# Second half of a mixing layer moved from the table loop into the edge batches, on one Trainium2 core

## The chip, the cores and the metric

The kernel runs on one core of one Trainium2 chip. The metric is device time in microseconds (us) from the launch to the end of the program, as the median of several runs. Engines: PE is TensorE, DVE is VectorE, ACT is ScalarE, POOL is GpSimd, SP is SyncE, which here only issues transfers. Each engine runs its own instructions in order and waits on semaphores for the others.

## The reference

One layer of a graph network over 3125 nodes of 256 numbers and 50,000 edges, everything in fp32. With xn the layer-normed nodes:

- A graph attention: keys, values and queries by node type (6 types), a score for each edge, a softmax over all edges of a type, and a sum of the weighted values into each target node, then a layer norm.
- A mixing layer ("mix") on the same xn: q, k and v by one weight, elu(q)+1 and elu(k)+1, linear attention over all nodes; then

```python
x1 = layer_norm(t + x, ln1_g, ln1_b)
h = gelu(x1 @ W1.T + b1)
y = h @ W2.T + b2
return layer_norm(y + x1, ln2_g, ln2_b)
```

- The sum of x and both goes through a layer norm and a feed-forward block (256 to 1024 to 256) whose output counts only for the top 1561 nodes by a router weight.

The change is about the four lines of code above. All of it is computed as before in both kernels.

## The kernel before, in words

Nodes stand in NT = 25 tiles of 128 rows; sorted by type and padded they fill NS = 30 tiles. Edges stand in 98 groups of 4 x 128; two groups are a batch, so there are 49 batches.

The program has five stages, all of them written out by hand: each engine has one list of calls, and the order of the calls in that list is the order of its work. There is no planner.

1. Front (0 to 80 us): loads, the first layer norm, keys of the mix layer, edge indices turned.
2. Table loop (80 to about 290 us), 31 steps. Step s computes keys, values and queries of sorted tile s (`turn_in`, `keys_values`, `queries`, `by_type` on PE; POOL gathers the tile's rows and scatters two tables), and beside that one tile of the mix layer, skewed over six steps: `mix_q`, `mix_t`, `mix_turn` (L996), `mix_h` (L985), gelu on ACT (L794), `mix_y` (L1006, L1007), then `residual` and `finish` on DVE. `turn_in` (L896) and `queries` (L932) write the same PSUM bank, `ps[0]`, so `turn_in` of the next tile waits until DVE has read the queries (L1252). SP stores the finished rows to `mix_scratch`.
3. Edge batches (about 300 to 918 us). For a batch: POOL gathers 8 x 128 rows of keys and values (L1425) into a ring of 7 slots of four tiles, the seventh of which is the memory of the mix weights, `wmix`; a slot is free again when `window_sums` has read it. SP loads query windows (L1384) and key rows (L1393). ACT builds one-hot matrices (L1485, L1488, L1500, L1504), copies sums (L1522, L1528) and takes the exponentials (L1513). PE: `target_rows` (L1604), `window_sums` (L1621), `turn_sums` (L1630), `turn_maxima` (L1648), `spread_maxima` (L1655), `totals` (L1639). DVE: `products` (L1750), `head_sums` (L1757), maxima, `weights` (L1800), `messages` (L1809), and one step of a search over nodes (L1853).
4. Combine (918 to 984 us): stored sums are scaled (L2062) and multiplied (L2315), chunks are stored and gathered back.
5. Feed-forward, selection and output (984 to 1167 us): PE L2351 and L2364; DVE prepares rows two tiles at a time in `normalise_pair`, reading `rows`, which were loaded from `mix_scratch`.

In the edge stage one iteration of the PE list is, in order: target_rows, turn_sums, turn_maxima, window_sums, spread_maxima, turn_sums, totals, target_rows, window_sums. The functions that the change touches, with the lines of the profile:

Of the kernel before, what the change touches and what calls it, by code (L numbers as in the profile page):

```python
# [15 lines left out]
P = 128  # L16
N, D = 3125, 256
C = D // P
# [14 lines left out]
RING = 7  # L33
RING_BIG = RING - 1
# [9 lines left out]
SEARCH_AT = 6  # L44
SEARCH_STEPS = 4 + NT + 4
# [11 lines left out]
STATS_AT = (13, 14, 15)  # L57
T_AT = 1
# [17 lines left out]
def build(nc, a, out):  # L76
# [6 lines left out]
    mix_d = scratch("mix_scratch", (NP, D))  # L83
    agg_d = scratch("agg_scratch", (AR, D))
# [5 lines left out]
    with ExitStack() as ctx:  # L90
# [27 lines left out]
        wqT, w1T, w2T = (wmix[:, i * C * D:(i + 1) * C * D].rearrange("p (c o) -> p c o", c=C) for i in range(3))  # L118
        vec_names = ["L0_gnn_ln_g", "L0_gnn_ln_b", "L0_mix_ln2_g", "L0_mix_ln2_b", "L0_mix_b2", "L0_ffn_b2",
# [33 lines left out]
        edge = Arena("edge", 7808)  # L153
# [70 lines left out]
        hT = big.take(2, D)  # L224
        assert big.at <= rel_end
        big.reset(xs_at)
        x2m = big.take(2, D)
        mo = big.take(2, D)
        den = big.take(2, H)
        sts, mvs, rss = big.take(4, 6), big.take(4, 2), big.take(4, 2)  # L230
        nmr = big.take(2)
        x1g = big.take(3, D)
# [16 lines left out]
        kv_slots = [kv[:, s, :, :] for s in range(RING_BIG)] + [wmix[:, :].rearrange("p (k d) -> p k d", k=EG)]  # L249
# [11 lines left out]
        gap = edge.take(4, 64)  # L261
        edge.reset()
# [24 lines left out]
        rows_c = edge.take(NT, D)  # L287
        selT = edge.take(C, ETY, P)
# [10 lines left out]
        junk = edge.take(NHG)  # L299
        edge.reset()  # L300
# [11 lines left out]
        same_t = [vecs[name][0:HW, 0:NHG] for name in ("L0_mix_ln2_g", "L0_mix_ln2_b")]  # L312
        base_f = vecs["L0_mix_b2"][:, 0:NHG + 1]
# [107 lines left out]
        def type_marks(c, dve, in_t, tmp):  # L421
            for t in range(ETY):
# [30 lines left out]
        m_q, m_min, m_exp, m_kf, m_t, m_tx, m_r1, m_rs, m_xh, m_T, m_x1, m_h, m_g, m_y, m_c, m_r2, m_out = (  # L453
            sem(n) for n in ("mix_q", "mix_min", "mix_exp", "mix_kf", "mix_t", "mix_tx", "mix_rstd_1", "mix_shift", "mix_xh",
                             "mix_turned", "mix_x1", "mix_h", "mix_gelu", "mix_y", "mix_stats_2", "mix_rstd_2", "mix_out"))
        m_xin = pair("mix_x_in")
        vmx, pmx, m_xg = sem("mix_step"), sem("mix_pool_step"), sem("mix_x1_gained")
        N_VEC = 5
        mix_vecs = ["L0_mix_b2", "L0_mix_ln2_g", "L0_mix_ln2_b", "L0_gnn_ln_b"]
        mix_vecs += [name for name in vec_names if name in ("L0_mix_ln1_g", "L0_mix_ln1_b")]  # L460
        late_vecs = [name for name in vec_names if name not in mix_vecs]
# [4 lines left out]
        with nc.Block() as block:  # L466
            @block.sync
            def _(sp):
# [80 lines left out]
                seen_all(sp, m_st, NT, 16)  # L549
                sp.wait_ge(s_late, 16 * N_LATE)  # L550
# [6 lines left out]
            def _(pool):  # L557
# [94 lines left out]
                def roots(t, ready, done, n):  # L652
                    if t is None:
                        return
                    seen(pool, ready, t)
                    j = 2 * n + t.k
# [3 lines left out]
                def gained(t):  # L660
                    if t is None:
                        return
                    if t.t == 0:
                        pool.wait_ge(s_pri, 1)
                    seen(pool, m_xh, t)
                    seen(pool, m_c, t.at(-3))
                    pool.tensor_tensor(x1g[:, t.t % 3, :], xh[:, t.k, :], vecs["L0_mix_ln1_g"][:, :], ALU.mult).then_inc(m_xg, 1)

                load(Tile(0, 0, NS))
                load(Tile(0, 1, NS))  # L670
                for s in range(NS + 1):
                    t, m = Tile(s // 2, s % 2, NS), Tile(s // 2, s % 2, NT)
                    roots(m.at(-5), m_c, m_r2, 1)
                    gained(m.at(-2))
                    load(t.at(2))
                    store_kv(t.at(0))
                    roots(m.at(-1), m_tx, m_r1, 0)
# [1958 lines left out]
```

## Time and profile before

| | us |
|---|---|
| median of three runs | 1170.04 |
| the three runs | 1173.99, 1167.43, 1170.04 |
| span of the profiled execution, its own time as far as the profile has it | 1167.3 |
| PE busy | 967.1 (83%) |
| DVE busy | 803.3 (69%) |
| POOL busy | 640.5 (55%) |
| ACT busy | 587.4 (50%) |

The span runs from the first to the last instruction of the profiled execution; the median of the timed runs is 2.7 us longer. Busy time is a sum over the whole span, so it hides that the stages differ: the profile's slices show PE full and at full clock in the table loop and in the feed-forward part, and at 0.5 to 0.7 of full clock in the edge batches.

### The profile page before, as it was taken

The numbers are of one execution on the slowest core, as the hardware profiler recorded it, in microseconds if no ns is written. First come the engines' busy times: TensorE is split into PE (matmuls) and PEld (weight loads), VectorE is DVE, ScalarE is ACT, GpSimd is POOL, SyncE is SP. The second block draws the span as 40 slices with busy tenths as digits, with TensorE's granted clock in tenths as the row PEclk, the third lists the DMA queues.
The fourth block names the chain that finished last, engine by engine and source line by source line (L and its number), as shares of the span: only waits on it lengthen the run. The fifth ranks groups of instructions, "written<-read, shape, count | busy, mean of one in ns | idle before, by whom it ended". The sixth has DMA issues, their size and how long they took to land.

```text
span 1167.3 us, 18084 instructions
## 1 busy us (share of the span) xinstructions
PE 967.1 (83%) x5053; PEld 677.5 (58%) x5053; DVE 803.3 (69%) x1708; ACT 587.4 (50%) x1534; POOL 640.5 (55%) x818
## 2 busy tenths in 40 slices
PE   5989999997157788777877878778778898999998
PEld 4767777775034444444444444444444687888886
DVE  7755888885256777777767677776767677887541
ACT  2657999983234554555545455554555322322220
POOL 4516788886725666666656666565664025664000
PEclk9999999999565766666667666666776799999999
DMA  9722544444736776766767767677674274210020
GB/s 294 220 71 104 159 145 145 146 146 174 234 114 182 208 212 210 205 204 203 214 202 214 210 198 211 201 211 208 201 211 146 69 226 152 79 46 19 1 86 25
DMA packets 112091, 189.89 MB, mean 163 GB/s; under 512 B 18187, under 2 KB 80734, under 8 KB 111990
## 3 DMA queue, kind: packets, MB, share of 16 engines
q0 software_dynamic: 38992, 129.87, 36.1%
q1 hardware_dynamic: 69718, 55.57, 15.7%
q10 hardware_dynamic: 3280, 3.28, 0.8%
q8 instruction: 43, 0.70, 0.2%
q14 instruction: 58, 0.48, 0.1%
HBM read 154.21 MB, written 34.44 MB: 162 GB/s over the span
## 4 chain that ended last, share of the span: by engine, by line
PE 55%; ACT 12%; issue 11%; another core or an unknown queue 10%; DVE 9%; DMA 1%; SPq 1%; POOL 0%; DVEq 0%; ACTq 0%; POOLq 0%
PE ps L2364 7%; PE ps L1621 7%; PE ps L2351 7%; PE ps L1604 6%; PE ps L921 4%; ACT edge L1500 4%; PE ps L2315 3%; PE ps L932 2%; PE ps L909 2%; PE ps L960 2%; ACT edge L1488 2%; PE ps L985 2%; ACT edge L1485 1%; PE ps L1639 1%
## 5 line engine op out<-in xcount | busy, mean ns | idle before, releaser
L1425 POOL DMA_INDIRECT big<-kv_scratch,src_i x336 | 317.8, 946 | 203.0 <-issue 89.8
L1604 PE MATMUL ps<-edge 64*128 64x256 f32 x784 | 177.6, 595 | 39.0 <-issue 38.8
L1750 DVE TENSOR_TENSOR big<-big,ps 128x1024 f32<-128x1024 f32 x84 | 101.6, 1210 | 121.3 <-PE ps L1604 61.9
L1621 PE MATMUL ps<-big,edge 128*64 128x256 f32 x672 | 149.4, 590 | 19.3 <-issue 10.3
L1604 PEld LDWEIGHTS ps<-edge 64*128 64x128 f32 x784 | 104.7, 289 | 89.5 <-issue 75.1
L1522 ACT ACTIVATE edge<-ps 128x256 f32<-128x256 f32 x98 | 37.6, 383 | 213.3 <-remote 146.0
L1621 PEld LDWEIGHTS ps<-big,edge 128*64 128x64 f32 x672 | 63.2, 199 | 78.6 <-issue 70.0
L1500 ACT ACTIVATE edge<-edge 128x64 f32<-128x64 f32 x392 | 102.9, 334 | 0.0
L1757 DVE TENSOR_REDUCE ps<-big 128x32 f32<-128x1024 f32 x84 | 102.3, 1218 | 0.1
L1809 DVE TENSOR_TENSOR big<-big,ps 128x1024 f32<-128x1024 f32 x84 | 98.9, 1209 | 0.0
L2351 PE MATMUL ps<-big 128*128 128x256 f32 (+2 forms) x416 | 88.7, 368 | 2.8 <-ACT big L2264 2.8
L2364 PE MATMUL ps<-big 128*128 128x256 f32 (+1 forms) x400 | 90.0, 380 | 0.0
L2277 ACT ACTIVATE big<-ps,fb 128x256 f32<-128x256 f32 (+2 forms) x104 | 39.4, 461 | 99.8 <-PE ps L2351 99.8
L1630 PE MATMUL ps<-ident,edge 128*128 128x128 f32 x196 | 53.6, 365 | 41.2 <-ACT edge L1522 32.7
L2351 PEld LDWEIGHTS ps<-big 128*128 128x128 f32 x416 | 74.3, 190 | 11.8 <-ACT big L2264 2.7
L2364 PEld LDWEIGHTS ps<-big 128*128 128x128 f32 (+1 forms) x400 | 73.6, 188 | 10.6 <-issue 0.3
L1425 POOL DMA_INDIRECT wmix<-kv_scratch,src_i x56 | 53.1, 948 | 30.8 <-issue 15.0
L1488 ACT ACTIVATE edge<-edge,ones 128x256 f32<-128x256 f32 x98 | 49.8, 508 | 29.4 <-remote 20.3
L1630 PEld LDWEIGHTS ps<-ident,edge 128*128 128x128 f32 x196 | 23.4, 168 | 68.7 <-ACT edge L1522 51.3
L921 PE MATMUL ps<-big,edge 128*128 x120 | 56.9, 596 | 0.5 <-ACT edge L727 0.3
L1485 ACT ACTIVATE edge<-edge,iota_n 128x256 f32<-128x256 bf16 x98 | 48.7, 497 | 13.9 <-DMA edge<-key_scratch 13.8
L1504 ACT ACTIVATE edge<-edge,ones 128x256 f32<-128x256 f32 x98 | 49.8, 508 | 8.9 <-issue 0.4
(354 smaller groups left out, 1919.0 us busy)
## 6 DMA issues: line engine op xcount, KB each, us to landing
edge<-q_scratch SPq DMA_DIRECT2D x196, 64.0 KB
edge<-key_scratch SPq DMA_DIRECT2D x98, 64.0 KB
big<-kv_scratch,src_i POOLq DMA_INDIRECT x336
agg_scratch<-big SPq DMA_DIRECT2D x16, 252.0 KB
xn_scratch<-big ACTq DMA_DIRECT2D x5, 640.0 KB, 5.4
mix_scratch<-big SPq DMA_DIRECT2D x25, 128.0 KB
big<-xn_scratch SPq DMA_DIRECT2D x25, 128.0 KB, 2.6
edge<-in_x SPq DMA_DIRECT2D x24, 128.0 KB
```

The lines of the kernel that those rows point to most:

```text
L921: ins = pe.matmul(ps[1][:, :], xgT[:, t.k, ch * P:(ch + 1) * P], wall[:, ds(ty, 1), ch, 0:2 * D].rearrange("p a o -> p (a o)"), start=(ch ...
L1425: pool.indirect_dma_start(kv_slots[s][:, k, :], None, kv_d[0:N, :], bass.IndirectOffsetOnAxis(ap=src_i[:, e:e + 1], axis=0)).then_inc(got[ ...
L1488: act.activation(ohT[:, g % 2, :], dist, ACT.Relu, bias=ones[:, 0:1], scale=-1.0).then_inc(oh, 1)
L1500: ins = act.activation(gap[:, 2 * k + hg, :], iota_m, ACT.Abs, bias=neg_key[:, e:e + 1])
L1604: ins = pe.matmul(qr_ps[g % 2][:, (2 * hg + k) * D:(2 * hg + k + 1) * D], ohT[64 * hg:64 * hg + 64, g % 2, k * P:(k + 1) * P], qwin[64 * h ...
L1621: ins = pe.matmul(sums_of(g)[64 * hg:64 * hg + 64, :], oneh[:, s, k, hg * 64:hg * 64 + 64], kv_slots[s][:, 2 * hg + k, D:2 * D], start=(k ...
L1630: ins = pe.transpose(sums_of(g)[:, ch * P:(ch + 1) * P], rows_of_sums(g)[:, ch * P:(ch + 1) * P], ident[:, :])
L1750: dve.tensor_tensor(k_rows, k_rows, qr_ps[g % 2].rearrange("p (k d) -> p k d", d=D), ALU.mult).then_inc(pr, 1)
L1757: dve.tensor_reduce(scr[:, g // 2 % 2, (g % 2) * EG * H:(g % 2 + 1) * EG * H].rearrange("p (k h) -> p k h", h=H), kv_slots[g % RING][:, :, ...
L1809: dve.tensor_tensor(v, v, wgt[:, g // 2 % 2, (g % 2) * EG * H:(g % 2 + 1) * EG * H] .rearrange("p (k h d) -> p k h d", h=H, d=1).to_broadc ...
L2351: ins = pe.matmul(hslot[q % 2][:, j * GT * P:j * GT * P + w], fw1[:, ch, f * P:(f + 1) * P], cols[:, ch, at:at + w], start=(ch == 0), stop ...
L2364: ins = pe.matmul(ps[4 + t % 2][0:m, 0:D], fh[:, p % 2, f, at:at + m], fw2[:, f, :], start=(f == 0), stop=(f == FJ - 1))
```

## The change

- The second half of the mix layer (W1, gelu, W2, residual, second statistics) leaves the table loop. Instead SP stores x1, turned, to a new scratch tensor `x1_d`, one tile per step; `mo` is now only x plus a bias.
- In the edge stage each of the 25 tiles is spread over four iterations. Tile m starts at b = 7 + 3m//2: ACT issues the load of x1 one iteration before, PE does `mix_h` at b, ACT the gelu at b+1, PE `mix_y` at b+1 (now with the residual added by a product with the identity), DVE a row, statistics, variance and gain at b+1, ACT issues the store to `x2_d` at b+2.
- The mix weights stay in `wmix`, so the gather ring has 6 slots and not 7.
- In the table loop `turn_in` gets its own bank, `ps[7]`, and stands right behind `keys_values`; `queries` now waits for DVE's read instead. On DVE `attend` stands ahead of `q_bias_in`. POOL's `gained` and the second `roots` go, and its loads run three tiles ahead.
- In the combine stage POOL takes 25 reciprocal roots at once; SP loads the rows of `x2_d`, and DVE adds them with one instruction per tile, `prepare_row`.

```diff
-RING = 7
-RING_BIG = RING - 1
+RING = 6
+RING_BIG = RING
+MIX_FROM = [7 + 3 * m // 2 for m in range(NT)]
+X1_LAG, X2_LAG = -1, 2
...
 SP, table loop
+                    seen(sp, m_x1, t)
+                    sp.dma_start(x1_d[t.t, :, :], x1T[:, t.t % 3, :]).then_inc(m_x1st[t.k], 16)
...
 PE, table loop
-                    seen(pe, g_qc, t.at(-1))
+                    seen(pe, g_Tc, t.at(-1))
-                        ins = pe.transpose(ps[0][...], xg[...], ident[:, :])
+                        ins = pe.transpose(ps[7][...], xg[...], ident[:, :])
...
                     keys_values(t.at(0))
+                    turn_in(t.at(1))
                     mix_t(m.at(-1))
                     mix_turn(m.at(-2))
                     queries(t.at(0))
-                    mix_h(m.at(-3))
-                    turn_in(t.at(1))
                     by_type(t.at(-1))
-                    mix_y(m.at(-4))
...
 ACT, edge batches
+                def load_x1(m):
+                    at_least(act, yp, m - 1)
+                    act.dma_start(x1e[:, m % 2, :], x1_d[m, :, :]).then_inc(x1in[m % 2], 16)
+                def store_x2(m):
+                    act.wait_ge(yg, m + 1)
+                    act.dma_start(x2_d[m * P:(m + 1) * P, :], x2e[:, m % 2, :]).then_inc(x2st[m % 2], 16)
+                def mix_gelu(m):
+                    act.wait_ge(hp, m + 1)
+                    at_least(act, yp, m)
+                    for j in range(C):
+                        ins = act.activation(hTe[...], h_ps_e[...], ACT.Gelu, bias=b1c[:, j:j + 1])
+                    ins.then_inc(hk, 1)
...
                         distances(2 * b + 2)
+                    for m in mix_tiles(b, X1_LAG):
+                        load_x1(m)
+                    for m in mix_tiles(b, 1):
+                        mix_gelu(m)
+                    for m in mix_tiles(b, X2_LAG):
+                        store_x2(m)
                     keep_rows(2 * b - 3)
...
 PE, edge batches
+                def mix_h(m):
+                    pe.wait_ge(x1in[m % 2], 16 * (m // 2 + 1))
+                    at_least(pe, yr, m)
+                    (4 products of 128 x 128 x 128 into h_ps_e)
+                def mix_y(m):
+                    pe.wait_ge(hk, m + 1)
+                    (2 products of 128 x 128 x 256 and 4 of 128 columns into y_ps_e)
...
                     turn_sums(2 * b - 3)
+                    for m in mix_tiles(b, 1):
+                        mix_y(m)
                     totals(b - 1)
                     target_rows(2 * b + 2)
                     window_sums(2 * b - 2)
+                    for m in mix_tiles(b, 0):
+                        mix_h(m)
...
 DVE, edge batches
+                def mix_row(m):
+                    dve.wait_ge(yp, m + 1)
+                    at_least(dve, x2st[m % 2], 16 * (m // 2))
+                    dve.tensor_tensor(x2e[:, m % 2, :], y_ps_e, vecs["L0_mix_b2"][:, :], ALU.add).then_inc(yr, 1)
...
                     mark(b)
+                    mix_row(m)      (m of mix_tiles(b, 1))
                     messages(2 * b - 2)
+                    mix_stats(m)
                     messages(2 * b - 1)
+                    mix_var(m)
+                    mix_gain(m)
...
 DVE, combine and feed-forward
+                def prepare_row(i):
+                    dve.wait_ge(s_x2r, 2)
+                    dve.wait_ge(mix_in[i // 2 % 3], 16 * (i // 6 + 1))
+                    dve.wait_ge(x2in[i % 2], 16 * (i // 2 + 1))
+                    dve.scalar_tensor_tensor(rows[:, i, :], x2e[:, i % 2, :], x2r[:, i:i + 1], rows[:, i, :], ALU.mult, ALU.add)
```

## Rows read from the trace of the kernel before

**Rows 1.** Busy time by stretch: us, then PE, PEld, DVE, ACT, POOL, clock, DMA share, GB/s.
```profile
177.43:249.91 72.48, 72.48 (x482) 57.74 (x481) 59.84 (x171) 67.65 (x130) 58.34 (x80) 1.00 0.41 146
418.00:890.00 472.00, 373.91 (x1679) 207.88 (x1677) 343.75 (x505) 249.96 (x743) 295.36 (x313) 0.66 0.70 207
984.00:1100.00 116.00, 113.76 (x554) 99.33 (x553) 85.90 (x291) 33.26 (x90) 58.67 (x104) 1.00 0.15 45
```
**Rows 2.** PE timeline, one step of the table loop: start, us, instruction, count.
```profile
202.28 1.06 PE L985 MATMUL ps<-big,wmix 128*128 128x128 f32 x8
203.18 0.43 PE L896 MATMUL ps<-ident,edge 128*128 128x128 f32 x2
...
204.38 0.70 PE L1006 MATMUL ps<-wmix,big 128*128 128x256 f32 x2
...
205.35 1.05 PE L960 MATMUL ps<-big,wmix 128*128 128x128 f32 x8
```
**Rows 3.** Groups by line, ten steps of the table loop (177.43 to 249.91).
```profile
L658 POOL TENSOR_TENSOR big<-big,nhalf 128x1 f32<-128x1 f32 x20 | 12.7, 637 | 1.7
L642 POOL DMA_INDIRECT kv_scratch<-edge,big x10 | 11.9, 1189 | 3.1 <-issue 3.1
L667 POOL TENSOR_TENSOR big<-big,v_L_mix_ln_g 128x256 f32<-128x256 f32 x10 | 7.2, 716 | 0.0
L1308 DVE SCALAR_TENSOR_TENSOR big<-big,v_L_mix_ln_g 128x256 f32<-128x256 f32 x10 | 4.5, 455 | 0.0
```
**Rows 4.** ACT timeline of the same step: the gelu and the table load before it.
```profile
203.16 1.28 ACT L794 ACT_TABLE_LOAD   x1
204.46 0.63 ACT L794 ACTIVATE big<-ps,b1c 128x128 f32<-128x128 f32 x2
```
**Rows 5.** Timeline of an early step, before the loop holds mix_h and mix_y.
```profile
89.27 0.44 PE L896 MATMUL ps<-ident,edge 128*128 128x128 f32 x2 [0.73 <-DVE edge L1252]
```
**Rows 6.** DVE timeline: first instruction of batches 8, 47 and 48.
```profile
418.13 1.22 DVE L1750 TENSOR_TENSOR big<-big,ps 128x1024 f32<-128x1024 f32 x1 [2.55 <-remote]
...
889.64 1.22 DVE L1750 TENSOR_TENSOR big<-big,ps 128x1024 f32<-128x1024 f32 x1 [2.99 <-PE ps L1604]
...
898.30 1.21 DVE L1750 TENSOR_TENSOR big<-big,ps 128x1024 f32<-128x1024 f32 x1
```
**Rows 7.** Who waited for whom, 418 to 890: us in total, times, longest.
```profile
DVE big L1750 <- PE ps L1604: 60.3, 20, 3.8
...
DVE big L1750 <- remote: 35.5, 14, 3.1
```
**Rows 8.** Timeline of batch 10, all engines (start, us, instruction, idle before).
```profile
444.72 0.51 ACT L1488 ACTIVATE edge<-edge,ones 128x256 f32<-128x256 f32 x1
...
445.50 0.38 ACT L1522 ACTIVATE edge<-ps 128x256 f32<-128x256 f32 x1 [0.27 <-issue]
...
446.54 0.36 ACT L1513 ACTIVATE edge<-edge 128x192 f32<-128x192 f32 x1 [0.66 <-issue]
...
447.39 1.13 PE L1604 MATMUL ps<-edge 64*128 64x256 f32 x8
...
448.11 2.33 DVE L1809 TENSOR_TENSOR big<-big,ps 128x1024 f32<-128x1024 f32 x2
...
450.37 0.41 DVE L1853 SCALAR_TENSOR_TENSOR edge<-v_L_mix_b,edge,step_f 128x196 f32<-128x196 f32 x1
...
454.15 1.22 DVE L1750 TENSOR_TENSOR big<-big,ps 128x1024 f32<-128x1024 f32 x1 [3.36 <-PE ps L1604]
```
**Rows 9.** Timeline at the end of batch 25, PE at full clock.
```profile
631.59 1.13 PE L1604 MATMUL ps<-edge 64*128 64x256 f32 x8
...
632.22 0.95 POOL L1425 DMA_INDIRECT big<-kv_scratch,src_i  x1 [0.30 <-issue]
...
635.53 0.44 PE L1630 MATMUL ps<-ident,edge 128*128 128x128 f32 x2 [2.81 <-ACT edge L1522]
```
**Rows 10.** One transfer issued from ACT, in the front: ns, min/median/max.
```profile
L694 ACTq DMA_DIRECT2D xn_scratch<-big x5: 366/382/440, 27.0 to 64.8; - x5
```
**Rows 11.** DVE timeline in the combine stage: one instruction of `gained`, then the next scale.
```profile
963.81 0.48 DVE L2429 SCALAR_TENSOR_TENSOR big<-big,v_L_gnn_ln_g 128x256 f32<-128x256 f32 x1
964.21 2.26 DVE L2062 TENSOR_TENSOR big<-big 128x756 f32<-128x756 f32 x2
```

More of the change, by code:

```diff
@@ L57 @@
 STATS_AT = (13, 14, 15)
+X2_AT = (14, 15)
 T_AT = 1
@@ L261, in build @@
         gap = edge.take(4, 64)
+        base_f = edge.take(NHG + 1)
+        hTe = edge.take(D)
+        x2s = edge.take(6)
+        assert edge.at <= NT * D + 32
         edge.reset()
@@ L287, in build @@
         rows_c = edge.take(NT, D)
+        edge.take(32)
         selT = edge.take(C, ETY, P)
@@ L299, in build @@
         junk = edge.take(NHG)
+        same_last = edge.take(NHG)
         edge.reset()
@@ L786, in affine @@
                     ins.then_inc(m_x1, 1)
-                def gelu(t):
-                    if t is None:
-                        return
-                    seen(act, m_h, t)
-                    seen(act, m_y, t.at(-2))
-                    for j in range(C):
-                        ins = act.activation(hT[:, t.k, j * P:(j + 1) * P], ps[7][:, j * P:(j + 1) * P], ACT.Gelu,
-                                             bias=b1c[:, j:j + 1])
-                    ins.then_inc(m_g, 1)
                 for s in range(NS + 1):
@@ L801, in _ @@
                     elu(m.at(0))
+                    weights(t.at(1))
+                    turn_in(t.at(1))
                     affine(m.at(-2))
-                    weights(t.at(1))
-                    gelu(m.at(-3))
-                    turn_in(t.at(1))
                     q_out(t.at(-1))
@@ L929, in queries @@
                     seen(pe, g_w, t)
+                    seen(pe, g_qc, t.at(-1))
                     for o in range(C):
@@ L1369, in build, with mix_tiles @@
             fac_ps = [ps[7][:, 0:ETY * NB], ps[0][:, 0:ETY * NB]]
+            h_ps_e, y_ps_e = ps[0][:, 0:D], ps[0][:, D:2 * D]
+            def mix_tiles(b, lag):
+                return [m for m in range(NT) if MIX_FROM[m] + lag == b]
             def in_range(g):
@@ L2035, in build @@
                 "scaled_first", "scaled_second", "rows_ps", "rows_kept"))
-            ck_st, mix_in = pair("rows_stored"), sem("mix_in")
+            ck_st, mix_in = pair("rows_stored"), [sem(f"x_rows_in{j}") for j in range(3)]
+            x2in, rp = pair("x2_in"), sem("rows_prepared")
+            s_x2r = sem("x2_rstds")
             s_fw, s_head, s_tails = sem("ffn_weights_in"), pair("heads_in"), pair("tails_in")
@@ L2132, in _ @@
                 load_part(1)
+                for i in range(2):
+                    sp.wait_ge(x2st[i], 16 * ((NT + 1 - i) // 2))
+                load_x2(0)
+                load_x2(1)
                 for k in range(NU):
@@ L2164, in _ @@
                 sp.wait_ge(s_totalst, 32)
-                for t in range(GR, NT):
-                    load_xn(t)
+                for t in range(4, NT):
+                    if t + 4 >= GR and t + 4 < NT:
+                        load_xn(t + 4)
+                    load_x2(t)
                 for t in range(NT):
```

177 lines of the change are left out of this document (94 added, 83 removed).

## The prediction

> **What bounds the kernel now.** I read the slices of the page first, then busy time by stretch, then for each stage a timeline of one step, and last who waited for whom.
>
> The table loop is bound by PE. In ten steps, 72.48 us, PE is busy for all 72.48 at clock 1.00, so a step costs 7.25 us; ACT has 67.65 and DVE and POOL about 59 each [rows 1]. Whatever leaves PE there shortens the step until the next engine is full.
>
> The edge batches are not bound by any engine. From batch 8 at 418.13 to batch 47 at 889.64 a batch takes 471.51 / 39 = 12.09 us [rows 6], with PE busy 79%, DVE 73%, POOL 63% and ACT 53% of the stretch [rows 1]. In a batch DVE runs without a break from its first product (batch 10: 442.04, that is 12.1 before 454.15) to the search step at 450.37 + 0.41, and then sits idle 3.36 us [rows 8]. Over the stretch these waits are 60.3 + 35.5 us [rows 7], about 2.5 us a batch. What DVE waits for is strange: target_rows started at 447.39 and took 1.13 us, so it was done at 448.5, yet DVE went on only at 454.15 [rows 8]. PE's speed is not it: in batch 25 PE ran at the higher of its two clock levels, its last product was done at 631.59 + 1.13 = 632.7, and it idled 2.81 us until ACT freed it at 635.5 [rows 9]. What ends at that time is the gathers: the last one was issued at 632.22, 2.9 us earlier. And batch 47, when the last gathers are out, takes 898.30 - 889.64 = 8.66 us [rows 6]. So a batch has about 3 us in which DVE and ACT have nothing to do, and PE's signals seem to be seen late as long as gathers are under way. That slack is the cover for the moved work, and the prediction turns on how much of the work fits under it.
>
> The feed-forward part is bound by PE again (113.76 of 116 us), with DVE at 85.90 [rows 1].
>
> **The table loop.** mix_h occupies PE from 202.28 to 203.18, 0.90 us; mix_y from 204.38 to 205.35, 0.97 us [rows 2]. Together 1.87 us of 7.25, which leaves 5.38. Would another engine be fuller than that? POOL: 5.83 a step [rows 1], less 0.72 for the gain, 0.64 for a root and 0.25 (estimate, the addition before it) is 4.2, and with three gaps like the 0.31 behind each indirect transfer [rows 3] 5.1: just under. ACT: 6.77 less two table loads of 1.28 and the gelu's 0.63 [rows 4] (there is no second table left in the loop, so the load back to exp goes too) is 3.6. DVE: 5.98 less four instructions of about 0.45 [rows 3] and smaller ones is under 4. So PE stays the bound, near 5.4; I take 5.5, because POOL is so close. That is 1.75 for each of the 21 steps that hold both parts, 37 us. The first four steps hold neither, but PE idles 0.73 us there waiting for DVE's read of the shared bank [rows 5]; its own bank ends that: 3 us. Of the last steps, which hold the tail of the mix layer, four lose 1.87 us of PE, but there POOL's scatters are close: I take 5. Sum -45. Bounds: -30, if POOL holds the step at 6.1; -53, if PE is all there is. The extra store of x1 lies on SP, which has its queue otherwise for one load and one store a step; nothing, up to 2.
>
> **The edge batches: where the work goes.** Of three batches, two hold a mix_h and two a mix_y. The iteration with mix_y is the dear one, for everything in it is one chain. I put it on batch 10, whose first product is at 442.04:
>
> - ACT is free at 444.72 + 0.51 = 445.23 [rows 8]. Now a table load 1.28, the gelu 0.63 [rows 4], one transfer issued, 0.38 [rows 10] (the load of x1 or the store of x2): 447.5. Then keep_rows, 0.38, done 447.9 instead of 445.88; then the table load back, 1.28, and the exponentials 0.36: done at 449.55 instead of 446.90 [rows 8]. So 2.65 us late, and weights and messages stand behind them on DVE.
> - PE: turn_sums waits for keep_rows, 448.4. mix_y is 0.97 and its four products with the identity half of mix_h, 0.45: 1.4 at full clock, 449.8; at the lower level 2.8, 451.2. totals, target_rows and window_sums are queued behind it, and POOL's next gathers behind window_sums.
> - DVE: weights and mark end about 450.3; mix_row waits for mix_y. Then mix_row 0.46, first message 1.17, statistics 0.46, second message 1.17, variance 0.2, gain 0.46, search 0.41: 4.3 us. Next product at 454.6 (full clock) or 455.6 (lower level), against 454.15 now.
>
> So if signals came at once, such a batch would cost 0.5 to 1.5 us, because the 3.36 us of idle time hide the rest. But mix_y stands exactly ahead of totals and target_rows, whose signals reach nobody before 454 [rows 8]. If DVE saw mix_y as late as it now sees target_rows, at 454.0, the 4.3 us would start there: 458.3, or 4.2 us more. The two ends are 0.5 and 4.2 us per tile. I take 2.4, about the middle: the nearest row (target_rows) is for the high end, but the turn_sums just ahead of mix_y is seen in time to let ACT go on in the same batch. 25 x 2.4 = 60 us; bounds 12 and 105.
>
> The page on the table load has a different price. By the rows the gelu starts 1.30 us after its table load [rows 4]. The Trainium skill, ScalarE: Activation LUTs, What ACT_TABLE_LOAD costs, gives about 1380 ns of drain on top of the 1283 ns for every switch; by that rule two switches a tile would bring exponentials 2.76 us later still, and 25 tiles 69 us more. The trace shows no such drain between the two instructions, and the sum goes by the trace.
>
> mix_h stands behind the last window_sums and ahead of target_rows, whose result DVE needs only 3 us into the next batch: 0.9 to 1.8 us of PE, in the stretch in which PE has work left or idles for signals. I take 0.3 a tile, 7 us; bounds 0 and 45 (all of it on the chain). Stores and loads of 128 KB, three a tile, ride beside 207 GB/s [rows 1]; counted in the same term. The ring of 6: a gather is released by the same window_sums as now, one group nearer to its use. Its product comes at least 2 us after it lands in steady batches, so nothing; up to 5 us in the first batches.
>
> **After the batches.** prepare_row is one more DVE instruction of 0.48 us [rows 11] per tile. Three stand between scales of the combine stage, where DVE is on the chain: 1.4. In the feed-forward part DVE goes from 85.90 to about 85.90 + 16 x 0.48 = 93.6 of 116 us [rows 1]: it fits, with some waits: 2. Sum 3; bounds 1 and 10.
>
> **Sum.** -45 + 60 + 7 + 3 = +25 us on the span's 1167.3, 1192; the median of the runs is 2.7 above the span: 1195.
>
> **Rivals.**
>
> 1. The slack takes it all (the side on which it is faster). Signals of mix_y come at once, batches with mix_y cost 0.8 us and the next batch gives half back, since POOL's gathers restart before DVE: 25 x 0.6 = 15, mix_h nothing. 1170 - 45 + 15 + 3 = 1143; with less luck 1155. For it: 95.8 us of DVE waits in the stretch [rows 7]; ACT idle for half of it. Against it: the chain ACT, PE, DVE in the iteration is serial and already fills the slack with nothing over. It decides from 1.4 us a tile down.
> 2. mix_y is seen only when the gathers have landed: 25 x 4.2 = 105, so 1170 - 45 + 105 + 7 + 3 = 1240. For it: target_rows in every steady batch. Against it: turn_sums, two instructions ahead, is not held so long.
> 3. The table loop doesn't shrink as it should (POOL's order with three transfers and one root pair, or the DVE read that queries now waits for): gain 20 and not 45, 1220. Against it: no engine but PE is over 5.1.
> 4. The page's drain at each table switch: 1264. Against it: the trace.
>
> **How the numbers follow.** A measurement of this kernel can't tell less than about 0.5% (6 us) from no change. Forecast 0.47 (its own range 1160 to 1225: 0.01 of it faster, 0.06 within 0.5%, 0.40 slower); rival 1 0.30 (0.26 faster, 0.04 within); rival 2 0.16; rival 3 0.05; rival 4 0.02, all slower. Faster 0.27, same 0.10, slower 0.63. The range must reach into rivals 1 and 2: 1145 to 1245.
>
> **What would show it.** The step of the table loop between 5.3 and 5.6 us with PE still full and only one or no ACT table load in it. In the batches: periods of 12.1 for iterations without mix_y and 13.5 to 16 for those with it; exponentials about 2.7 us later there; DVE's idle time in front of L1750 gone and new idle time in front of mix_row, on mix_y. If mix_row waits until the last gather has landed, rival 2 is right. If batches stay at 12.1 to 12.6 throughout, rival 1 is. The forecast is wrong if the edge stage grows by less than 35 us.

## The result, and the profile after

The changed kernel takes 1154.84 us (median of 4 runs, 1152.96 to 1161.79) against 1168.74 for the kernel before on the same chip: ratio 0.9891, 95% interval 0.9859 to 0.9923. It is 1.1% faster, where 1195 was forecast. The profiled execution has a span of 1151.2 us against 1167.3. A second measurement on another chip (below) gave 0.9876, 0.9826 to 0.9925. Executions over 1.5% above the fastest of the same kernel are left out of the ratios, so a ratio can differ a little from the quotient of two medians.

The table loop first. One step is the distance between two `keys_values` (PE timeline: start, us, instruction, count), and the first row below is ten steps by stretch, as [rows 1].

```profile
133.87:188.29 54.42, 54.42 (x361) 40.89 (x361) 36.93 (x111) 37.66 (x90) 39.59 (x51) 1.00 0.62 218
```
```profile
139.15 1.88 PE L913 MATMUL ps<-big,edge 128*128 x4
140.87 0.38 PE L888 MATMUL ps<-ident,edge 128*128 128x128 f32 x2
144.59 1.88 PE L913 MATMUL ps<-big,edge 128*128 x4
146.31 0.38 PE L888 MATMUL ps<-ident,edge 128*128 128x128 f32 x2
```
The step is 5.44 us (was 7.25), and PE is still busy for all of it.

Then where the edge batches begin in the two kernels: batch 0 of before, then batches 0, 8, 26 to 29, 47 and 48 of after (DVE timeline). Batch 26 holds mix_y and mix_h (yh), 27 mix_y only (y), 28 mix_h only (h), and so on in threes.

```profile
301.86 1.22 DVE L1750 TENSOR_TENSOR big<-big,ps 128x1024 f32<-128x1024 f32 x1 [0.80 <-issue]
```
```profile
252.10 1.22 DVE L1765 TENSOR_TENSOR big<-big,ps 128x1024 f32<-128x1024 f32 x1 [0.50 <-issue]
...
363.01 1.22 DVE L1765 TENSOR_TENSOR big<-big,ps 128x1024 f32<-128x1024 f32 x1 [2.32 <-remote]
...
595.17 1.22 DVE L1765 TENSOR_TENSOR big<-big,ps 128x1024 f32<-128x1024 f32 x1 [1.96 <-remote]
...
608.89 1.22 DVE L1765 TENSOR_TENSOR big<-big,ps 128x1024 f32<-128x1024 f32 x1
...
620.80 1.22 DVE L1765 TENSOR_TENSOR big<-big,ps 128x1024 f32<-128x1024 f32 x1
...
632.05 1.22 DVE L1765 TENSOR_TENSOR big<-big,ps 128x1024 f32<-128x1024 f32 x1 [2.50 <-remote]
...
858.93 1.22 DVE L1765 TENSOR_TENSOR big<-big,ps 128x1024 f32<-128x1024 f32 x1 [3.56 <-PE ps L1594]
...
870.92 1.22 DVE L1765 TENSOR_TENSOR big<-big,ps 128x1024 f32<-128x1024 f32 x1 [2.79 <-remote]
```
From batch 8 to 47 a batch takes (858.93 - 363.01) / 39 = 12.72 us, against 12.09 [rows 6]. The three in the middle take 13.72 (yh), 11.91 (y) and 11.25 (h). Over batches 8 to 43 the means of the twelve of each kind are 15.0, 12.7 and 10.5: a yh batch costs 2.9 us more than a batch of before, a y batch 0.6 more, and the h batch that ends the three is 1.6 us shorter than one. (One yh batch, 14, takes 19.9; with a ring of 6 it is long also without the moved work, 15.9 and 16.0. Without it the yh mean is 14.5.)

DVE's time splits these 24.4 us (495.92 against 471.51) by simple subtraction. DVE is busy for 379.4 us of this stretch and was for 343.4: 36.0 more, 1.4 a tile. Its idle time fell only from 128.1 to 116.5. In front of `products` it fell from 108 to 15 us, but new waits took its place: 17 us in front of mix_row, 19 in front of the reduction that waits for the exponentials (L1815), 18 in front of `maximum` (L1801), and most, 45, in front of `subtract`, which waits for PE's `spread_maxima`. The largest part of those (363 to 859: us, times, longest):
```profile
DVE edge L1808 <- remote: 25.3, 14, 2.3
```
By kind, DVE is idle 4.4 us in a yh batch, 2.5 in y and 1.8 in h, against 3.3 in a batch of before.

Last, what the combine stage waits for. These are PE's first combine matmul in before and in after, DVE's longest total wait in that stage of after (us, times, longest), and the rows of DVE and SP around its two stalls.

```profile
920.71 0.55 PE L2315 MATMUL ps<-bd_m,big 128*126 128x128 f32 x1 [1.45 <-DVE big L2062]
```
```profile
892.25 0.97 PE L2374 MATMUL ps<-bd_m,big 128*126 128x128 f32 x3 [1.45 <-DVE big L2102]
```
```profile
DVE edge L2495 <- DMA wmix<-mix_x_scratch: 13.8, 2, 8.9
```
```profile
939.25 0.50 SPq L2160 DMA_DIRECT2D wmix<-mix_x_scratch  x1
...
944.39 0.48 DVE L2495 SCALAR_TENSOR_TENSOR edge<-wmix,v_L_mix_ln_b,edge 128x256 f32<-128x256 f32 x1 [4.92 <-DMA wmix<-mix_x_scratch]
...
964.95 0.42 SPq L2160 DMA_DIRECT2D wmix<-mix_x_scratch  x1
...
967.23 0.48 DVE L2495 SCALAR_TENSOR_TENSOR edge<-wmix,v_L_mix_ln_b,edge 128x256 f32<-128x256 f32 x1 [8.87 <-DMA wmix<-mix_x_scratch]
```
`prepare_row` waits for its x2 rows, and SP issues their load only at 939.25 and 964.95, because the loads stand in its queue behind stores and waits for totals. From the first combine matmul to the end it is 1151.2 - 892.25 = 259.0 us, against 1167.3 - 920.71 = 246.6.

So the 16.1 us by which the span is shorter are made up as follows: the first product comes 49.8 us earlier; batches 0 to 7 take 5.4 less (116.3 to 110.9); batches 8 to 46 take 24.4 more; batch 47 to the first combine matmul 2.3 more (31.1 to 33.3); the rest 12.4 more.

### The profile page after: what moved, and what is told of

Its sections match the earlier page's. It is cut to its first block, busy times and chain, and to the rows that moved or that the text cites. A ratio compares the mean times of both kernels' runs of the same rounds, so it can differ in the third digit from the quotient of the medians.

```text
span 1151.2 us, 18271 instructions
## 1 busy us (share of the span) xinstructions
PE 925.1 (80%) x5153; PEld 678.8 (59%) x5153; DVE 790.9 (69%) x1682; ACT 598.7 (52%) x1540; POOL 600.2 (52%) x745
## 4 chain that ended last, share of the span: by engine, by line
PE 45%; DVE 17%; issue 14%; ACT 10%; POOL 5%; another core or an unknown queue 4%; DMA 3%; SPq 1%; DVEq 0%; ACTq 0%; POOLq 0%
PE ps L1611 7%; PE ps L1594 5%; PE ps L2423 5%; PE ps L913 4%; PE ps L2410 4%; DVE big L1824 4%; PE ps L954 2%; PE ps L2374 2%; PE ps L925 2%; PE ps L901 2%; ACT edge L1466 2%; DVE big L1765 2%; POOL big L2272 2%; PE ps L1620 2%
## 5 line engine op out<-in xcount | busy, mean ns | idle before, releaser
L1389 POOL DMA_INDIRECT big<-kv_scratch,src_i x392 | 370.9, 946 | 257.5 <-PE ps L1611 120.8
L1594 PE MATMUL ps<-edge 64*128 64x256 f32 x784 | 145.2, 501 | 35.3 <-issue 22.5
L1611 PE MATMUL ps<-big,edge 128*64 128x256 f32 x784 | 138.1, 485 | 31.0 <-issue 13.8
L1765 DVE TENSOR_TENSOR big<-big,ps 128x1024 f32<-128x1024 f32 x98 | 118.5, 1209 | 44.1 <-remote 34.5
L1594 PEld LDWEIGHTS ps<-edge 64*128 64x128 f32 x784 | 86.6, 238 | 62.1 <-issue 50.2
L1772 DVE TENSOR_REDUCE ps<-big 128x32 f32<-128x1024 f32 x98 | 119.4, 1218 | 0.1
L1824 DVE TENSOR_TENSOR big<-big,ps 128x1024 f32<-128x1024 f32 x98 | 116.6, 1208 | 0.0
L1620 PE MATMUL ps<-ident,edge 128*128 128x128 f32 x196 | 49.5, 341 | 70.3 <-ACT edge L1488 60.9
L2410 PEld LDWEIGHTS ps<-big 128*128 128x128 f32 x416 | 77.8, 201 | 12.5 <-ACT big L2323 2.7
L1454 ACT ACTIVATE edge<-edge,ones 128x256 f32<-128x256 f32 x98 | 49.8, 508 | 23.9 <-remote 10.4
L2374 PE MATMUL ps<-bd_m,big 128*126 128x128 f32 (+1 forms) x396 | 49.3, 289 | 7.9 <-DVE big L2102 6.9
L1808 DVE TENSOR_TENSOR edge<-edge,ps 128x192 f32<-128x192 f32 x49 | 17.2, 351 | 55.4 <-remote 31.0
```

The lines of the kernel that those rows point to most:

```text
L1389: pool.indirect_dma_start(kv_slots[s][:, k, :], None, kv_d[0:N, :], bass.IndirectOffsetOnAxis(ap=src_i[:, e:e + 1], axis=0)).then_inc(got[ ...
L1594: ins = pe.matmul(qr_ps[g % 2][:, (2 * hg + k) * D:(2 * hg + k + 1) * D], ohT[64 * hg:64 * hg + 64, g % 2, k * P:(k + 1) * P], qwin[64 * h ...
L1611: ins = pe.matmul(sums_of(g)[64 * hg:64 * hg + 64, :], oneh[:, s, k, hg * 64:hg * 64 + 64], kv_slots[s][:, 2 * hg + k, D:2 * D], start=(k ...
L1620: ins = pe.transpose(sums_of(g)[:, ch * P:(ch + 1) * P], rows_of_sums(g)[:, ch * P:(ch + 1) * P], ident[:, :])
L1765: dve.tensor_tensor(k_rows, k_rows, qr_ps[g % 2].rearrange("p (k d) -> p k d", d=D), ALU.mult).then_inc(pr, 1)
L1772: dve.tensor_reduce(scr[:, g // 2 % 2, (g % 2) * EG * H:(g % 2 + 1) * EG * H].rearrange("p (k h) -> p k h", h=H), kv_slots[g % RING][:, :, ...
```

## The experiments

The kernel before had medians between 1168.6 and 1177.5 us beside these runs, so all comparisons are between ratios to it; 0.01 is 12 us. The changed kernel's own is 0.989 and 0.988.

**The yardstick.** The changed kernel, unedited, run late in the series.

> The changed kernel once more, unedited, beside the same runs of the kernel before, as the yardstick for the ratios of the other experiments. If the ratio does not depend on the chip it is 0.989 (0.986 to 0.992); if it does, the comparisons of the experiments with the changed kernel shift by the difference.

Measured: 0.9876 (0.9826 to 0.9925). The ratio holds, and the interval says that less than about 6 us can't be told between two experiments.

**The x2 loads earlier.**
```
-X2_AT = (14, 15)
+X2_AT = (13, 14, 16)
...
-                    load_x2(t)
+                    if t >= 2 + len(X2_AT):
+                        load_x2(t)
```


> The changed kernel, with the loads of the stored x2 rows of tiles 2, 3 and 4 issued earlier on SP's queue (behind the stores of units 13, 14 and 16, ahead of the waits for head rows and totals). In the changed kernel DVE stands still 4.92 us from 939.5 and 8.87 us from 958.4 waiting for exactly these loads. Theory A (those two stalls are the 12 us by which the part behind the batches grew): both go, 10 to 14 us faster, about 1142. Theory B (the gathers of sums or POOL's roots are as late as the loads, so another wait takes their place): 0 to 3 us faster, 1152 to 1155.

Measured: 1148.96, ratio 0.9735 (0.9699 to 0.9772), 16 to 18 us faster than the changed kernel by the ratios, 12 to 14 by the medians (1148.96 / 1175.85 = 0.977). DVE's waits for these loads over the same stretch of the profile:
```profile
DVE edge L2496 <- DMA wmix<-mix_x_scratch: 5.8, 2, 3.3
```
They fell from 13.8 to 5.8, and the part behind the first combine matmul (at 898.43 of a span of 1147.8) from 259.0 to 249.4, 2.8 us over the 246.6 of before. Theory A. The profiles show 9.6 us of the gain; the rest is within what the intervals leave open. It is the version with the lowest ratio that leaves nothing out.

**The moved work left out of the batches.**
```
             def mix_tiles(b, lag):
-                return [m for m in range(NT) if MIX_FROM[m] + lag == b]
+                return []
```


> The changed kernel with the moved second half left out of the edge batches altogether (no loads of x1, no products, gelu, row work or stores; the combine stage reads other rows of the same size in place of x2). Theory A (the moved work costs what the batches grew, 12.72 - 12.09 = 0.63 us a batch): batches of 12.1 us, about 25 us faster, 1130. Theory B (the moved work does cost 2.4 us a tile, 60 us, as forecast, and something else in the changed kernel made the batches shorter at the same time, such as the clock that rose from 0.66 to 0.80): batches of 10.5 to 11.2 us, 50 to 70 us faster, about 1095.

Measured: 0.9689 (0.9663 to 0.9715), 23 us faster than the changed kernel. Its batches 8 and 47 begin at:
```profile
362.28 1.22 DVE L1765 TENSOR_TENSOR big<-big,ps 128x1024 f32<-128x1024 f32 x1 [2.69 <-PE ps L1594]
...
844.27 1.22 DVE L1765 TENSOR_TENSOR big<-big,ps 128x1024 f32<-128x1024 f32 x1 [3.83 <-PE ps L1594]
```
That is 12.36 us a batch, against 12.87 for the kernel with earlier x2 loads on the same chip. Theory A: the moved work really costs only 0.9 us a tile net, with whatever the changed clock gives back in it, and no other part of the change hid a larger price.

**The ring alone, in the kernel before.**
```
-RING = 7
-RING_BIG = RING - 1
+RING = 6
+RING_BIG = RING
```
(and the slot in `wmix` taken off the list.)

> The kernel before with a ring of six gathered groups in place of seven, and nothing else. Theory A (the ring only sets when the last gathers fall): batches stay at 12.09 us, the one in which the last gathers land moves by one (batch 47 12 us and not 8.66): 3 to 4 us slower, about 1172. Theory B (the ring of six is itself what lengthened the batches by 0.63 us): 20 to 25 us slower, about 1192.

Measured: 0.9993 (0.9974 to 1.0012). Batches of 12.29 us, and the last one with gathers takes 11.96 us, not 8.66, as A says; on the whole time even that can't be seen. On the same chip the changed kernel without the moved work had 12.36. Theory B is out.

**Half the gathers, before and after.**
```
-                    for k in range(EG):
+                    for k in range(0, EG, 1 if g < RING else 2):
...
-                    dve.wait_ge(got[u], 64 * (g // RING + 1))
+                    dve.wait_ge(got[u], 64 + 32 * (g // RING))
```


> The kernel before with every second gather of the edge batches left out after the first seven groups (POOL issues 4 a batch in place of 8, 1.25 us each; the rows that are left stay from earlier groups). In the run with plain copies for the gelus four different results of PE became visible together at 572.9, 2.0 us after the last gather had been issued. Theory A (PE's signals are held back while gathers are under way, and that sets the period of 12.1 us): batches of about 8.7 us, as the one batch behind the last gathers, 130 us faster, about 1040. Theory B (the 12.1 us have to do with something else, PE's work at its lower clock level or the key and query windows that SP loads): 11 to 12 us a batch, less than 45 us faster.

Measured: 1036.44, ratio 0.8817 (0.8779 to 0.8855), 139 us faster. Theory A. Its batches 8 and 47:
```profile
397.94 1.22 DVE L1750 TENSOR_TENSOR big<-big,ps 128x1024 f32<-128x1024 f32 x1
...
757.41 1.20 DVE L1750 TENSOR_TENSOR big<-big,ps 128x1024 f32<-128x1024 f32 x1
```
9.22 us a batch, and DVE is busy for 342.7 of these 359.5 us, 95%: now DVE is the bound. The run takes two things away at once, though: 5.0 us of POOL's own issuing a batch (four gathers, 1.25 us apart) and the late signals. In the kernel before, POOL's round adds up to the period: eight gathers from 442.27 to 451.96, then 2.42 us until the next starts, 12.1 in all (rows in the last section). How much of the 2.9 us is due to the late signals and how much to the issuing is not separated by any run.

And the changed kernel with the same gathers gone:

> The changed kernel with the same gathers left out. Theory A (a slack that the gathers make hides the moved work): without that slack every tile costs what its instructions take in the chain, 1.5 us on DVE and up to 2.6 us of later exponentials, 40 to 100 us over the 25 tiles, so this kernel comes out level with or slower than the one before with half its gathers, although its table loop is 50 us shorter. Theory B (the moved work costs 0.5 to 0.6 us a batch whatever the gathers do): 15 to 20 us faster than that one.

Measured: 1085.55, ratio 0.9242 (0.9204 to 0.9280): 50 us slower than the one above, though its table loop is 50 us shorter. First products of batches 8, 24 (y), 25 (h), 26 (yh), 27 and 47:
```profile
344.27 1.22 DVE L1765 TENSOR_TENSOR big<-big,ps 128x1024 f32<-128x1024 f32 x1
...
535.22 1.22 DVE L1765 TENSOR_TENSOR big<-big,ps 128x1024 f32<-128x1024 f32 x1
...
546.26 1.22 DVE L1765 TENSOR_TENSOR big<-big,ps 128x1024 f32<-128x1024 f32 x1
...
555.04 1.22 DVE L1765 TENSOR_TENSOR big<-big,ps 128x1024 f32<-128x1024 f32 x1
...
569.20 1.22 DVE L1765 TENSOR_TENSOR big<-big,ps 128x1024 f32<-128x1024 f32 x1
...
795.15 1.21 DVE L1765 TENSOR_TENSOR big<-big,ps 128x1024 f32<-128x1024 f32 x1
```
A mean of 11.56; y takes 11.04, h 8.78, yh 14.16. Without the slack the moved work costs (11.56 - 9.22) x 39 / 25 = 3.7 us a tile. With it, 1.0. Note that a yh batch takes about the same in both, by the medians 14.2 here and 14.3 with all gathers, while y and h batches have 11.2 and 8.8 here and 12.8 and 11.0 there. So the full gathers lengthen the y and h batches and hardly the yh ones. That a yh batch is one chain over the engines is my reading of it.

**The table loads, with and without the slack.**
```
-   ins = act.activation(hTe[...], h_ps_e[...], ACT.Gelu, bias=b1c[:, j:j + 1])
+   ins = act.activation(hTe[...], h_ps_e[...], ACT.Copy)
```


> The changed kernel with a plain copy in place of the gelu in the edge batches, so that ACT needs no other table there: the same instructions in the same places, two table loads of 1.28 us a tile less, and exponentials 2.6 us earlier in 25 batches. Theory A (the exponentials stand on the chain of a batch with mix_y, and the slack hides about half): 1.0 to 1.5 us a tile, 25 to 35 us faster, that is all of what the moved work costs. Theory B (DVE's own extra 1.5 us is what lengthens the batch, and the exponentials' lateness lies beside it): 0 to 8 us faster.

Measured with all gathers: 0.9901 (0.9864 to 0.9937), no gain at all.

> The changed kernel with every second gather left out and with plain copies in place of the gelus (no table loads in the edge batches). With all gathers the missing table loads gained nothing. Theory A (they lie on the chain of a batch and were hidden only by the gathers): 2.0 to 2.6 us a tile, 50 to 65 us faster than with half the gathers and the gelus, 1020 to 1035. Theory B (they lie beside DVE's work in any case): 0 to 15 us faster, 1070 to 1085.

Measured with half the gathers: 1039.42, ratio 0.8832 (0.8804 to 0.8859), 48 us faster than with the switches, 1.9 us a tile. The price is close to that of theory A (1.9 where it had 2.0 to 2.6), and the copies, 0.43 us for two against 0.63, are a small part of it. So in the first of the two B had the right number but not the reason: the loads are on the chain, and with all gathers something else takes their place. The trace of the kernel without switches shows what, in its yh batch that begins at 560.99:
```profile
567.07 1.06 PE L1669 MATMUL ps<-ident,wmix 128*128 128x128 f32 x4
...
569.97 0.94 POOL L1389 DMA_INDIRECT big<-kv_scratch,src_i  x1 [0.30 <-issue]
...
572.94 0.42 DVE L1909 TENSOR_TENSOR wmix<-ps,v_L_mix_b 128x256 f32<-128x256 f32 x1 [3.78 <-remote]
```
mix_y is done at 568.1 and mix_row starts at 572.94, 2.0 us behind the issue of the last gather. POOL had issued eight gathers without a break since 561.22. That is not every tile: of the 25 mix_row, DVE idled for "remote" ahead of five, 19.1 us in all, against one and 4.1 us in the changed kernel. In the changed kernel, with its table loads, the same place looks like this (batch 23, which begins at 557.02):
```profile
562.90 1.28 ACT L1510 ACT_TABLE_LOAD   x1
...
564.20 0.63 ACT L1510 ACTIVATE edge<-ps,b1c 128x128 f32<-128x128 f32 x2
564.21 0.35 DVE L1808 TENSOR_TENSOR edge<-edge,ps 128x192 f32<-128x192 f32 x1 [1.19 <-PE ps L1645]
...
564.40 0.95 POOL L1389 DMA_INDIRECT big<-kv_scratch,src_i  x1 [1.55 <-PE ps L1611]
...
566.29 0.61 PE L1670 MATMUL ps<-ident,wmix 128*128 128x128 f32 x4
566.41 0.36 ACT L1479 ACTIVATE edge<-edge 128x192 f32<-128x192 f32 x1
...
567.36 0.41 DVE L1910 TENSOR_TENSOR wmix<-ps,v_L_mix_b 128x256 f32<-128x256 f32 x1
567.69 1.21 DVE L1824 TENSOR_TENSOR big<-big,ps 128x1024 f32<-128x1024 f32 x1
```
mix_y is done at 566.9 and mix_row runs at 567.36, behind `mark`, with no wait of its own. POOL is issuing here too, but in a shorter run: it had paused until 564.40 for window_sums. By kind, the kernel without switches has 15.2, 12.1 and 12.0 where the changed one has 15.0, 12.7 and 10.5: the y batch gains, and the h batch gives back nothing any more.

**DVE's four steps spread.** mix_row behind the second messages; statistics, variance and gain in the next batch, ahead of `maximum`, `subtract` and `weights`; `X2_LAG` 3; with the earlier x2 loads.

> The changed kernel with the earlier x2 loads, and with DVE's four steps of a tile moved: mix_row behind the second messages of the batch, statistics, variance and gain into the next batch, each ahead of an instruction for which DVE stands idle there (maximum, subtraction, weights). Nothing is left out. Theory A (what a tile costs is DVE's own 1.5 us in a batch that DVE fills, and messages that stand behind a late signal of mix_y): batches of 12.4 to 12.6 us, 8 to 18 us faster than with the earlier loads alone, 0.96 of the time of before. Theory B (the cost is PE's work or the chain over the gelu ahead of the exponentials): within 3 us of the kernel with the earlier loads alone, 0.973.

Measured: 0.9754 (0.9705 to 0.9802), within 0.002 of the same without it; batches of 13.05 in the profile, whose execution was the longest of the six (1159.07). Not DVE's order, then, as theory B says, within the 6 us or so that the intervals leave open.

**Both edits together.**

> The kernel with the earlier x2 loads and DVE's steps spread, now also with plain copies for the gelus, so without table loads in the edge batches. Each of these two edits alone gained nothing with all gathers. Theory A (they cover for one another: without table loads the messages stood up to 3.8 us behind a late signal of mix_y, as at 572.94; with mix_row behind the messages that wait is off the chain): batches of 12.3 to 12.5 us, as with the moved work left out, 15 to 25 us faster than the spread kernel, ratio 0.955 to 0.962. Theory B (what is left of the cost has another cause, such as PE's work or late signals of target_rows and window_sums, which come later the more PE has to do): batches of 12.9 to 13.1, ratio 0.972 to 0.977.

Measured: 1137.83, ratio 0.9734 (0.9691 to 0.9776). The profile has batches of 12.54 against 12.86 of the changed kernel on the same chip, close to the 12.3 to 12.5 of theory A, but the whole time is no better than with the x2 loads alone (0.9735), as B says. A profile is a single execution, so how much of the 0.3 us is real stays open. Its batch 26 shows what is left (the last gather, the last products and who waits for them):
```profile
596.04 1.08 PE L1610 MATMUL ps<-big,edge 128*64 128x256 f32 x8
596.72 0.95 POOL L1389 DMA_INDIRECT big<-kv_scratch,src_i  x1 [0.30 <-issue]
599.77 0.42 DVE L1909 TENSOR_TENSOR wmix<-ps,v_L_mix_b 128x256 f32<-128x256 f32 x1 [2.94 <-remote]
600.02 0.38 ACT L1488 ACTIVATE edge<-ps 128x256 f32<-128x256 f32 x1 [3.90 <-remote]
...
600.25 1.10 POOL L1389 DMA_INDIRECT big<-kv_scratch,src_i  x1 [2.59 <-remote]
```
window_sums is done at 597.1, and ACT and POOL, which both wait for it, go on at 600.0 and 600.25. mix_row, at 599.77, waits for mix_y, which was done at 594.8.

**The traffic.** Loads of x1 and stores of x2 only for the first two tiles.
```
-                        load_x1(m)
+                        if m < 2:
+                            load_x1(m)
```
(and `store_x2` alike, with the waits for them.)

> The changed kernel in which only the first two tiles of the edge batches load their x1 rows and store their x2 rows; 23 loads and 23 stores of 128 KB are left out, all products and DVE steps stay. Theory A (the 5.9 MB that the moved part adds to the traffic of the gathers are what lengthens the batches by 0.6 us): batches of 12.1 to 12.4 us, 12 to 20 us faster than the changed kernel. Theory B (the traffic fits; PE, ACT and DVE in the chain make the difference): within 4 us of the changed kernel, ratio 0.986 to 0.992.

Measured: 0.9882 (0.9846 to 0.9918). No effect; theory B.

**PE's products.** One matmul for four in mix_h, one for four in mix_y.

> The changed kernel with one matmul in place of four in mix_h, and one in place of four in mix_y; gelu, table loads, DVE steps, loads and stores stay. PE's share of a tile falls from 2.3 us at full clock (4 at the lower level) to 0.5. Theory A (PE's work ahead of target_rows and window_sums is what is left of the cost): yh batches of 12.5 to 13 us in place of 14.2, 12 to 20 us faster than the changed kernel. Theory B (ACT's detour is, or the waits for one another): 0 to 5 us faster.

Measured: 0.9846 (0.9809 to 0.9883), 0.003 to 0.0045 under the changed kernel, 4 to 5 us: less than the intervals can tell from nothing. Its batches have 12.91 us, no less than those of the changed kernel. Theory B.

**The bank, in the table loop.** `turn_in` back in `ps[0]` and behind `queries`, waiting for DVE's read of them.
```
-                        ins = pe.transpose(ps[7][...], xg[...], ident[:, :])
+                        ins = pe.transpose(ps[0][...], xg[...], ident[:, :])
...
                     keys_values(t.at(0))
-                    turn_in(t.at(1))
                     mix_t(m.at(-1))
                     mix_turn(m.at(-2))
                     queries(t.at(0))
+                    turn_in(t.at(1))
```


> The changed kernel with the turned rows of the table loop back in the bank that the queries use, and back behind the queries in PE's order. Theory A (the own bank is part of the 50 us that the table loop gave: without mix_h between them PE stands still 0.7 us a step until DVE has read the queries): a step of 6.1 to 6.2 us in place of 5.44, 15 to 22 us slower than the changed kernel. Theory B (the loop's gain is all the removed work, 1.87 us a step): a step of 5.4 to 5.5 us, within 3 us of the changed kernel.

Measured: 1245.66, ratio 1.0589 (1.0550 to 1.0629), 82 to 84 us slower than the changed kernel. A step is 7.82 us, far more than either theory had:
```profile
134.51 0.42 DVE L1219 TENSOR_TENSOR edge<-ps,big 128x256 f32<-128x256 f32 x1
```
```profile
134.99 0.44 PE L888 MATMUL ps<-ident,edge 128*128 128x128 f32 x2 [2.17 <-DVE edge L1219]
...
142.81 0.44 PE L888 MATMUL ps<-ident,edge 128*128 128x128 f32 x2 [2.17 <-DVE edge L1219]
```
The change had also moved this read of the queries (L1219) behind the steps of `attend`. That is harmless with the own bank and dear without it. So once more, with DVE's old order:
```
-                    attend(m.at(-1))
                     q_bias_in(t.at(0), ty)
+                    attend(m.at(-1))
```


> The changed kernel with the shared bank as in the run with turned rows behind the queries (a step of 7.82 us), but with DVE's read of the queries ahead of its four steps of attention, as in the kernel before. In the run with DVE's new order that read started at 134.51, 1.9 us after the queries were done, behind attend. Theory A (most of the 2.4 us a step came from that order, the bank alone costs the 0.73 us that PE idled in the early steps of before): a step of 6.1 to 6.3 us, about 40 us faster than that run, ratio to before 1.00 to 1.02. Theory B (the bank itself does it): a step of 7.5 us or more, ratio 1.05.

Measured: 1192.2, ratio 1.0114 (1.0084 to 1.0143), 26 to 28 us slower than the changed kernel.
```profile
116.08 0.44 PE L888 MATMUL ps<-ident,edge 128*128 128x128 f32 x2 [0.72 <-DVE edge L1219]
122.46 0.44 PE L888 MATMUL ps<-ident,edge 128*128 128x128 f32 x2 [0.72 <-DVE edge L1219]
```
A step of 6.38 us, with the same idle 0.7 as in the early steps of before [rows 5]. Theory A. Against 5.44 that is 0.94; PE's idle time explains 0.72 of it.

## Why the prediction was wrong

**The table loop** was right: step 5.44 for 5.5, 49.8 us for 45. But the credit was given to the wrong part. I gave 3 us to the own bank, since only the first four steps showed its wait. In the later steps mix_h stood between `queries` and `turn_in` and covered that wait; with mix_h gone it is open in every step. The bank, with the place of `turn_in` that it allows, is worth 26 to 28 of the 50 us, and without it the changed kernel is slower than before (1.0114).

**The edge batches** are the step that failed: "I take 2.4" us a tile for mix_y, 60 us, and 7 for mix_h. Measured are 24.4 us for both, 1.0 a tile (23 us by leaving them out). The working of one batch was not far off: 0.5 to 4.2 us, and a yh batch takes 2.9 more. Two things failed. First, I charged every tile with the price of a batch by itself and multiplied by 25. In threes the batches are 2.9 and 0.6 longer and 1.6 shorter: 1.75 for each batch with a mix_y, and 0.8 of that back in the h batch. In an h batch DVE is idle 1.8 us and not 3.3, and POOL has moved its gathers into the long batches: on average 8.9 of them start in a yh batch, 8.2 in y and 6.9 in h, where before every batch has eight. That the h batch is short because its gathers are already out is my reading; the counts and waits fit it. I had written a return into rival 1 and not into the sum. Second, I took the middle between two ends. The runs show that the chain's extra length and the late signals don't add, they cover for one another. Take the table loads away and late signals take their place (no gain); take half the gathers away and the same loads cost 1.9 us a tile, and the whole tile 3.7. Net, a tile costs 1.0 us where DVE alone got 1.4 us more to do, so by subtraction the slack took in what ACT and PE had more, and 0.4 of DVE's. Rival 1 had the right mechanism in the main, and its price of 0.6 a tile was 0.4 too low.

The sign that the prediction gave for being wrong was an edge stage that grows by less than 35 us. From the first product to the first combine matmul it grew by 21.3. Its picture of the waits held for the first products, but the new idle time is mostly in front of `subtract`, not of mix_row. Against the forecast span of 1192 the terms are off by 4.8 us in the table loop, 42.6 in batches 8 to 46, 5.4 in the batches ahead of them, for which nothing was forecast, all towards faster, and by 2.3 and 9.4 behind them towards slower. Also, the 95.8 us of waits [rows 7] leave out those of the products that read the seventh slot, in `wmix`; with them it is 110.7, 2.8 a batch.

**mix_h**, "0.3 a tile", can't be told apart from mix_y; with PE's products cut to a fraction at most 4 to 5 us came back for both.

**Signals of mix_y** (rival 2): as a rule they are seen at once in the changed kernel (566.9 to 567.36 in batch 23; of 25 mix_row one idled 4.1 us, the others 1.0 at most). The late signal exists, as 572.94 shows, and without the table loads it meets mix_y more often, five times.

**The ring of 6**: nothing that can be told, as forecast, up to the batch of the last gathers, which moved by one.

**After the batches** 3 us was forecast with 10 as bound, and 12.4 measured. The DVE instructions were counted; the loads that they wait for were not followed through SP's queue. With them moved ahead, 2.8 remain, the 3 of the forecast.

**The page's drain** (rival 4): the Trainium skill, ScalarE: Activation LUTs, What ACT_TABLE_LOAD costs, puts about 1380 ns of drain on top of the load. In the changed kernel the gelu starts 1.30 us after its table load starts (562.90, 564.20), and that load starts right behind the instruction ahead of it (562.38 + 0.51). Both switches of a tile together cost 1.9 us with half the gathers, less than the 2 x 1.28 of the loads alone. The trace does not agree with the page here.

What stays open: which path makes the last half microsecond a batch. Traffic, DVE's order, the ring and the table loads were each shown not to move it by themselves by more than the intervals, and PE's products by a few us at most. No run took only DVE's own 1.4 us a tile away. Why PE's results are seen late in a run of gathers is not known either.

## What to carry to other kernels

Where a stage's period is set by one engine's stream, here POOL's gathers, work added to some rounds is to be priced over the whole group of rounds: the stream can do more of its work during the long ones, and the short ones pay back. When an instruction is taken out, look at which wait it had covered, and whether the shared resource behind that wait must go too. Follow each new load to the queue that issues it, and read what stands ahead of it there.

## What was not expected of the hardware

When POOL issues eight gathers in a row without a pause, the results that PE finishes late in that run reach the other engines together, about 2 us after the last issue ends. The end of batch 10 in the kernel before:
```profile
451.01 0.95 POOL L1425 DMA_INDIRECT big<-kv_scratch,src_i  x1 [0.30 <-issue]
...
454.14 0.38 ACT L1522 ACTIVATE edge<-ps 128x256 f32<-128x256 f32 x1 [4.41 <-remote]
454.37 0.94 POOL L1425 DMA_INDIRECT big<-kv_scratch,src_i  x1 [2.42 <-remote]
```
The run began at 442.27. totals, done at 447.5, are read by DVE at 447.85, so results early in the run come at once. target_rows, done at 448.5, and window_sums, done at 451.3, are seen by DVE, ACT and POOL only between 454.14 and 454.37. Likewise 568.1 is seen at 572.94 without the table loads, and 597.1 at 600.0 to 600.25 in the run with both edits. ACT and POOL don't wait for gathered rows there, so the landing of the gathers doesn't explain it. With every second gather gone, window_sums done at 581.7 goes on in ACT at 581.72, and a batch falls from 12.1 to 9.2 us.

PE's clock rose although it got more to do. Stretches of 39 batches, first with the moved work left out, then of the changed kernel (columns as in [rows 1]):
```profile
362.28:844.27 481.99, 383.72 (x1677) 214.69 (x1677) 343.49 (x504) 249.56 (x741) 296.63 (x312) 0.64 0.69 202
```
```profile
363.00:859.00 496.00, 374.29 (x2077) 247.67 (x2077) 379.51 (x605) 330.07 (x842) 295.21 (x312) 0.81 0.72 210
```
The granted clock is 0.64 without it and 0.81 with it, and PE's busy time goes down from 383.7 to 374.3 us with a quarter more matmuls. So in PE's busy time the moved products were more than paid for. Whether that shortened the batches is not shown: in the kernel before, the 19 of these 39 batches with a granted clock under 0.6 take 12.05 us on average, no more than the 12.09 of all. The traces don't show why the clock rose; the run with PE's products cut short, which stands between the two in the number of matmuls, had 0.74 over its 39 batches.
